# Identity products in TensorE's waits, and a root of eight operations, in a kernel of delta-rule attention and routed experts

## The chip, the cores and the metric

The kernel runs on one core of one Trainium2 chip. The metric is the device time of one execution in microseconds (us), the median of three executions of the same program. The engines are called PE (TensorE matmul), PEld (its weight load), DVE (VectorE), ACT (ScalarE), POOL (GpSimd) and SP (SyncE, which issues DMAs). "Tensor clock" is the clock that the chip grants to TensorE, as the profile shows it: 1.00 is the upper of its two levels (2.4 GHz), 0.50 the lower (1.2 GHz).

## What is computed

A gated delta-rule attention layer over 8 sequences of 512 tokens, width 256, 8 heads of 128, with a small feed-forward behind it, then a layer of 8 experts whose tokens are assigned by 20 rounds of a balanced normalization (Sinkhorn) and of which each token takes two.

```python
# attention layer, x: (8, 512, 256)
q, k = l2norm(silu(h @ Wq)), l2norm(silu(h @ Wk))        # per head, 128 wide
v, beta = silu(h @ Wv), sigmoid(h @ Wb)
alpha = exp(-exp(A_log) * softplus(h @ Wa + dt_bias))
def step(S, t):                                          # S: 128 x 128 per head
    S = S * alpha[t]
    S = S + outer(k[t], (v[t] - k[t] @ S) * beta[t])
    return S, (q[t] @ S) * 128 ** -0.5
o = rms_norm(o) * o_norm_w * silu(h @ Wg)
x = x + o @ Wo
m = rms_norm(x)
x = x + square(relu(m @ W_fc)) @ W_proj
...
# expert layer on layernorm(x), 4096 tokens, 8 experts
la = -(xf @ gate_W.T) / 0.05
for _ in range(20):
    la = la - logsumexp(la, axis=-1, keepdims=True)
    la = la - logsumexp(la, axis=-2, keepdims=True)
pi = exp(la)
_, top_idx = top_k(pi, 2)
y = (silu(xf @ W_gate[e]) * (xf @ W_up[e])) @ W_down[e]
out = sum over k of y[top_idx[:, k]] * pi[:, k]
```

rms_norm, l2norm and layernorm each divide by a square root; the kernel works these out as inverse square roots on DVE and POOL.

## The kernel before

**Staging.** The 4096 tokens are 32 tiles of 128. Start-up loads and norms the input and prepares the decays. Then `step(t, p, more, ahead, tail)` runs once for each tile on every engine: it advances the recurrence of tile t (the "state" part), prepares tile f = t + 1 (the "front" part: projections, transposes, products of keys, the inverse of a triangular matrix in blocks) and finishes tile t - 1 (the "tail": output projection, feed-forward, logits of the gate). Steps 1 to 28 are a loop, the others stand unrolled. In the last step (TILES - 1) there is no next tile, so `more` and `ahead` are false; behind it the tail of tile 31 runs alone. Then come the balanced assignment and the routing (`pe_late`, `dve_late`, `act_late`, `pool_late`), and behind them 24 slots of expert work.

**What sets the order.** Each engine's program is written out by hand; every hand-over is a semaphore. PE runs its instructions in the order of its program, so a wait at one of them holds all behind it.

**The roots.** `root` (L1480) on DVE works out an inverse square root from an integer guess (L1482) and three Newton steps of three operations each (L1484 to L1486): ten operations, each of which waits for the one before (`ch.link`). `k_root` calls it in each step for the norms of the keys of tile f and, in the same instructions, for those of the outputs of tile t - 1; behind it on DVE stand `tail_o` (L1697: o_s times root times gate, which PE transposes at L1991), the scalars of the keys and `delta_products` (L1585: it frees the PSUM bank that PE's next products of keys at L1901 need). `newton` (L1161) does the same on POOL in seven operations for the two norms of a row (`m_root`, `x_root`). For tile 31 both are done by `root` on DVE.

**PE in the last step and after it.** L1957 is the products of the state, L1914, L1929, L1930, L1940 and L1951 the blocks of the inverse, L1991 and L2001 the output projection (tail_o, tail_wo), L2008 and L2018 the first layer of the feed-forward (tail_m, tail_fc), L2028 the second (tail_proj), L2035 and L2042 the logits (tail_xf, tail_logits).

**PE in the assignment and the routing** (`pe_late`). L773 and L775 spread column maxima; L778 is one product for each of the 20 rounds, with the column sums, and DVE does the round's other work (L526 to L531); L780 and L781 count tokens; L787 builds the list of entries in eight batches, from matrices that DVE (L609, L610) and ACT (L749) make; L790 turns it; L797 transposes the first gathered rows of the experts, and from L767 on the experts' products follow.

**Precision.** All these products are 32-bit: a product of `nc.tensor.matmul` on plain f32 data stands in the trace as two records, a transpose or a product of f32r data (L767, L2028) as one.

## Time and profile before

| | us |
|---|---|
| median of 3 runs | 2355.87 (2354.88 to 2356.85) |
| the profiled execution's own time | 2354.47 |
| its span in the trace | 2352.7 |
| PE busy, share of the span | 2130.1 (91%) |
| DVE busy | 1773.0 (75%) |
| ACT busy | 1052.1 (45%) |
| POOL busy | 687.8 (29%) |
| mean granted Tensor clock | 0.956 |

The span is the time from the first to the last instruction in the trace; the execution's own time is 1.8 us more. Busy time is how long an engine works, whatever waits for it; PE's busy time is modelled for pipelined matmuls. In timeline rows the first number is the start, the second how long the row's instructions take together, "x16" how many records they are, and the brackets at the end name the idle time before the row and what ended it.

### The profile page before, as it was taken

The page shows a single profiled execution, that of the slowest core. Times are in us where ns is not written, and L with a number is a line of the kernel's source. Part 1 is how long each engine was busy: PE and PEld are TensorE (multiplying, and loading weights), DVE is VectorE, ACT ScalarE, POOL GpSimd, SP SyncE. Part 2 cuts the span into 40 slices and gives each one's busy share as a digit, 9 for nine tenths or more (in the row PEclk, how much of TensorE's full clock was granted, in tenths as well). Part 3 has the DMA queues.
Part 4 walks back from the last instruction along what each step waited for, and adds up shares of the span by engine and source line. Part 5 has one row for each costly group of instructions (what it writes and reads, how often), then busy time and mean ns, then how long its engine had stood idle before and what let it go on. Part 6 is the DMA issues. An engine that isn't in the chain of part 4 may idle for free. (4 is left out here: it accounts for less than half of the span.)

```text
span 2352.7 us, 50334 instructions
## 1 busy us (share of the span) xinstructions
PE 2130.1 (91%) x16226; PEld 1895.0 (81%) x16226; DVE 1773.0 (75%) x4277; ACT 1052.1 (45%) x2216; POOL 687.8 (29%) x1092
## 2 busy tenths in 40 slices
PE   4679999999999999999999998613799999999998
PEld 4468888888888888888888887512699999999887
DVE  6678888888888888888888887377577666666653
ACT  2334454444444544444445443202455555555542
POOL 0113232332332323323323232000434443344332
PEclk9789999999999999999999999856899999999999
DMA  5321212222222122121221221001444545454331
GB/s 190 114 35 37 57 36 48 44 37 53 39 41 53 36 48 44 37 54 39 43 52 36 48 42 26 8 7 56 153 157 165 188 150 168 143 176 166 125 120 19
DMA packets 307783, 181.71 MB, mean 77 GB/s; under 512 B 244716, under 2 KB 286064, under 8 KB 298512
## 3 DMA queue, kind: packets, MB, share of 16 engines
q1 hardware_dynamic: 255184, 149.21, 22.2%
q0 software_dynamic: 11280, 29.31, 4.4%
q10 hardware_dynamic: 41264, 2.51, 1.1%
q8 instruction: 29, 0.48, 0.1%
q14 instruction: 26, 0.21, 0.0%
HBM read 150.23 MB, written 32.51 MB: 78 GB/s over the span
## 5 line engine op out<-in xcount | busy, mean ns | idle before, releaser
L631 DVE TENSOR_TENSOR w_lo<-w_raw,w_hi 128x512 fp32r<-128x512 f32 x288 | 190.2, 688 | 3.9
L767 PE MATMUL ps_back<-w_hi,eh_hi 128*128 128x256 f32 x624 | 180.0, 289 | 3.2 <-DVE eh_lo L641 3.2
L767 PE MATMUL ps_back<-w_lo,eh_hi 128*128 128x256 f32 x624 | 176.5, 283 | 0.0
L767 PE MATMUL ps_back<-w_hi,eh_lo 128*128 128x256 f32 x624 | 176.4, 283 | 0.0
L721 ACT ACTIVATE w_hi<-w_raw 128x512 fp32r<-128x512 f32 x288 | 169.5, 626 | 0.0
L733 ACT ACTIVATE sact<-ps_inva 128x512 f32<-128x512 f32 (+1 forms) x96 | 49.7, 517 | 236.3 <-PE ps_inva L767 207.1
L1284 ACT ACTIVATE v_s<-ps_front 128x512 f32<-128x512 f32 x64 | 38.1, 595 | 237.9 <-PE ps_front L767 237.9
L1284 ACT ACTIVATE g_s<-ps_front 128x512 f32<-128x512 f32 x64 | 38.2, 598 | 225.8 <-PE ps_front L767 215.8
L1901 PE MATMUL ps_front<-kqT_t 128*128 128x256 f32 x512 | 129.2, 396 | 8.9 <-DVE aP L1585 8.9
L767 PE MATMUL ps_inva<-xT_hi,w_hi 128*128 128x512 f32 (+1 forms) x384 | 135.2, 352 | 1.7 <-DVE xT_lo L636 1.7
L1957 PE MATMUL ps_back<-state,kqT_t 128*128 128x128 f32 x1024 | 132.4, 279 | 3.2 <-DVE r_s L1657 1.7
L767 PE MATMUL ps_inva<-xT_lo,w_hi 128*128 128x512 f32 (+1 forms) x384 | 134.9, 351 | 0.0
L767 PE MATMUL ps_inva<-xT_hi,w_lo 128*128 128x512 f32 (+1 forms) x384 | 134.6, 351 | 0.0
L767 PE MATMUL ps_invb<-xT_hi,w_lo 128*128 128x512 f32 (+1 forms) x384 | 134.2, 349 | 0.0
L767 PE MATMUL ps_invb<-xT_hi,w_hi 128*128 128x512 f32 (+1 forms) x384 | 134.1, 349 | 0.0
L767 PE MATMUL ps_invb<-xT_lo,w_hi 128*128 128x512 f32 (+1 forms) x384 | 134.1, 349 | 0.0
L1957 PEld LDWEIGHTS ps_back<-state,kqT_t 128*128 128x128 f32 x1024 | 126.8, 195 | 6.1 <-DVE r_s L1657 1.9
L659 DVE TENSOR_TENSOR eh<-sact,ps_inva 128x512 f32<-128x512 f32 (+1 forms) x96 | 56.4, 588 | 93.2 <-ACT sact L733 68.3
L2018 PE MATMUL ps_back<-rows,tails 128*128 128x128 f32 x1024 | 126.0, 283 | 0.5 <-ACT rows L1340 0.5
L1187 POOL TENSOR_SCALAR xrow_v<-bag 128x1 f32<-128x1 f32 x31 | 7.1, 228 | 406.7 <-DVE bag L1734 406.7
L1207 POOL TENSOR_TENSOR k_s<-k_s,dbh 128x1024 f32<-128x1024 f32 x32 | 60.7, 1896 | 222.4 <-DVE dbh L1576 222.4
L767 PE MATMUL ps_front<-wqk_hi,hT_hi 128*128 128x512 f32 x256 | 107.3, 419 | 18.9 <-ACT k_s L1284 13.4
(381 smaller groups left out, 6603.2 us busy)
## 6 DMA issues: line engine op xcount, KB each, us to landing
w_raw<-L_ffn_W_gate_dram SPq DMA_DIRECT2D x24, 1024.0 KB
w_raw<-L_ffn_W_up_dram SPq DMA_DIRECT2D x24, 1024.0 KB
w_raw<-L_ffn_W_down_dram SPq DMA_DIRECT2D x24, 1024.0 KB
dT<-alphaT_d SPq DMA_DIRECT2D x32, 512.0 KB, 3.7
x_all<-L_attn_x_dram SPq DMA_DIRECT2D x4, 1024.0 KB, 9.9
hTr<-hT_d SPq DMA_DIRECT2D x32, 128.0 KB, 3.7
lt_d<-aP SPq DMA_DIRECT2D x256, 8.0 KB, 1.5
xi<-low_d SPq DMA_DIRECT2D x32, 128.0 KB
```

The costliest lines, as they stand in the source:

```text
L631: V.tensor_tensor(piece(w_lo[p], m).bitcast(F32R), piece(w_raw, m), piece(w_hi[p], m), ALU.subtract).then_inc(split[n], 1)
L659: V.tensor_tensor(eh[:, s, 0:rows], sact[:, s, 0:rows], psG[2 * s + 1][:, 0:rows], ALU.mult).then_inc(eh_ready[s], 1)
L721: A(piece(w_hi[p], m).bitcast(F32R), piece(w_raw, m), ACT.Copy).then_inc(hi_ready[n], 1)
L733: A(sact[:, s, 0:rows], psG[2 * s][:, 0:rows], ACT.Silu).then_inc(sact_ready[s], 1)
L767: ins = MM(out_, w[a].bitcast(F32R), x[b].bitcast(F32R), start=start and n == 0, stop=stop and n == 2)
L1187: link(pool.tensor_scalar(xrow_v[:, 0:1], bag[:, 1:2], LN_EPS, None, ALU.add), x_pool, n)
L1207: pool.tensor_tensor(k, k, per_head(dbh[:, :]), ALU.mult).then_inc(kd_ready, 1)
L1284: A((k_s[:, q], q_s, v_s, g_s)[n // 2][:, n % 2 * GW:(n % 2 + 1) * GW], psF[u % 2][:, :], ACT.Silu).then_inc(front_evac[u % 2], 1)
L1901: last = MM(ps[:, h * 2 * P:(h + 1) * 2 * P], kqT[:, c, 0, :], kqT[:, c].rearrange("p a n -> p (a n)"), start=True, stop=True)
L1957: last = MM(ps[:, h * DK:(h + 1) * DK], left(g * HG + h), right(g * HG + h), start=True, stop=True)
L2018: last = MM(ps[:, fb * P:(fb + 1) * P], wfc[:, k, c:c + P], mT[:, k * P:(k + 1) * P], start=k == 0, stop=k == KD - 1)
```

## The change

`keep_busy(ps, n)` is new: n products of the identity matrix with itself, 128 x 128 by 128 columns in f32, written to a PSUM bank that nobody reads then. It is put at these places of PE's program, each time ahead of something that PE waits for: in the last step 8 products ahead of block_t, 6 ahead of half_t and 4 ahead of state_out; in tile 31's own tail 22 ahead of tail_o, 16 ahead of tail_m, 4 ahead of tail_proj and 14 ahead of tail_xf; 6 behind tail_logits; in the assignment 10 behind each round's product, 25 more behind the last; 60 behind L781; 35 ahead of the first rows of the experts. That is 400 products.

The root on DVE becomes eight operations instead of ten (another polynomial for the second step); start-up keeps the ten under the name `row_root`. POOL's root becomes six operations instead of seven. The counts of semaphores follow.

```diff
--- before.py
+++ after.py
@@ -59,7 +59,7 @@
 ROOT_MAGIC = 1597463007.0
 LOG_SPREAD = 69.0
 SPREAD = float(np.float32(np.exp(LOG_SPREAD)))
-NEWTON = -8192.0
+NEWTON = -256 / 3
 
 
 NBETA, GAM, GTOT, MEAN = (8 * n for n in range(4))
@@ -301,7 +301,7 @@
 
             return b_filled(s, u) + 1
 
-        N_NORM, N_ROW, N_M, N_O, N_LANE, N_PAIR, N_LATE = 13, 8, 6, 2, 13, 4, 33
+        N_NORM, N_ROW, N_M, N_O, N_LANE, N_PAIR, N_LATE = 11, 7, 5, 2, 13, 4, 27
         N_IDENT, N_ZEROED = 8, 13
         XB16, XB32 = NB16 - 2, NB32 - 1
         N_BLOCKS, N_XBLOCKS = NB16 + NB32, XB16 + XB32
@@ -761,6 +761,10 @@
             for p in range(2):
                 slot(SLOTS - 2 + p, p, BROWS, None if p else BROWS)
 
+        def keep_busy(ps, n):
+            for _ in range(n):
+                nc.tensor.matmul(ps[:, 0:P], ident[:, :], ident[:, :], start=True, stop=True)
+
         def exact(MM, out_, w, x, start, stop):
 
             for n, (a, b) in enumerate(((0, 0), (0, 1), (1, 0))):
@@ -776,9 +780,12 @@
             for n in range(ROUNDS):
                 pe.wait_ge(sk_dve, shares_at(n))
                 MM(col_sums(n), ones[:, :], cols_, start=True, stop=True).then_inc(cols_summed, 1)
+                keep_busy(psI[0][0], 10)
+            keep_busy(psI[0][0], 25)
             pe.wait_ge(rt_dve, 13)
             MM(V3(psF[0][:, 0:TE]), upper[:, :], both, start=True, stop=True).then_inc(rt_pe, 1)
             MM(V3(psF[1][:, 0:TE]), ones[:, :], both, start=True, stop=True).then_inc(rt_pe, 1)
+            keep_busy(psI[0][0], 60)
 
             for b in range(BATCH):
                 pe.wait_ge(lanes_ready, b + 1)
@@ -825,6 +832,7 @@
                     if r % RB == RB - 1:
                         last.then_inc(y_filled[r // RB], 1)
 
+            keep_busy(psI[0][0], 35)
             pe.wait_ge(te_ready, 1)
             rows_T(0, 0, BROWS, BB)
             with pe.Fori(0, SMALL) as i:
@@ -1160,16 +1168,11 @@
             def newton(v, r, a, chain, n):
 
                 first_root(v, r, chain, n + 1)
-                c = 1.0
-                for k in range(3):
-                    m = n + 2 * k + 1
-                    link(pool.tensor_scalar(a, r, r, v, ALU.mult, ALU.mult), chain, m + 1)
-                    last = pool.tensor_scalar(r, a, -3.0 * c * c, r, ALU.add, ALU.mult)
-                    if k < 2:
-                        link(last, chain, m + 2)
-                    c *= -2.0 * c * c
-                assert c == NEWTON
-                return last
+                link(pool.tensor_scalar(a, r, r, v, ALU.mult, ALU.mult), chain, n + 2)
+                link(pool.tensor_scalar(r, a, -3.0, r, ALU.add, ALU.mult), chain, n + 3)
+                link(pool.tensor_scalar(a, r, r, v, ALU.mult, ALU.mult), chain, n + 4)
+                link(pool.tensor_scalar(a, a, -40 / 3, a, ALU.add, ALU.mult), chain, n + 5)
+                return pool.tensor_scalar(r, a, 80.0, r, ALU.add, ALU.mult)
 
             def front_scalars_free(f):
                 pool.wait_ge(ss_ready, 2 * f + 1)
@@ -1185,7 +1188,7 @@
                 pool.sem_inc(pool_turn, 1)
                 n = N_ROW * t + 1
                 link(pool.tensor_scalar(xrow_v[:, 0:1], bag[:, 1:2], LN_EPS, None, ALU.add), x_pool, n)
-                link(newton(xrow_v[:, 0:1], xrow_r[:, 0:1], xrow_r[:, 1:2], x_pool, n), x_pool, n + 7)
+                link(newton(xrow_v[:, 0:1], xrow_r[:, 0:1], xrow_r[:, 1:2], x_pool, n), x_pool, n + 6)
                 pool.tensor_scalar(xrow_r[:, 0:1], xrow_r[:, 0:1], 1.0 / NEWTON, None, ALU.mult).then_inc(xr_ready, 1)
 
             def o_squares(t, p):
@@ -1209,7 +1212,7 @@
             def scaled_v(f):
                 for n in range(2):
                     pool.wait_ge(front_evac[n], f_evac(f, FU_V + n))
-                pool.wait_ge(norm_dve, N_NORM * f + 12)
+                pool.wait_ge(norm_dve, N_NORM * f + 10)
                 pool.sem_inc(pool_turn, 1)
                 pool.tensor_tensor(heads(vb), heads(v_s), per_head(sqk[:, :]), ALU.mult).then_inc(vb_ready, 1)
 
@@ -1480,11 +1483,22 @@
             def root(ch, v, r, a):
 
                 ch.link(V.tensor_scalar(r.bitcast(I32), v.bitcast(I32), -0.5, ROOT_MAGIC, ALU.mult, ALU.add))
+                ch.link(V.scalar_tensor_tensor(a, r, -0.1875, r, ALU.mult, ALU.mult))
+                ch.link(V.tensor_tensor(a, a, v, ALU.mult))
+                ch.link(V.scalar_tensor_tensor(r, a, 0.5625, r, ALU.add, ALU.mult))
+                ch.link(V.scalar_tensor_tensor(a, r, 64 / 9, r, ALU.mult, ALU.mult))
+                ch.link(V.tensor_tensor(a, a, v, ALU.mult))
+                ch.link(V.scalar_tensor_tensor(a, a, -10 / 3, a, ALU.add, ALU.mult))
+                ch.link(V.scalar_tensor_tensor(r, a, 5.0, r, ALU.add, ALU.mult))
+
+
+            def row_root(ch, v, r, a):
+
+                ch.link(V.tensor_scalar(r.bitcast(I32), v.bitcast(I32), -0.5, ROOT_MAGIC, ALU.mult, ALU.add))
                 for _ in range(3):
                     ch.link(V.scalar_tensor_tensor(a, r, -0.5, r, ALU.mult, ALU.mult))
                     ch.link(V.tensor_tensor(a, a, v, ALU.mult))
                     ch.link(V.scalar_tensor_tensor(r, a, 1.5, r, ALU.add, ALU.mult))
-
 
             PART = TILES // XPARTS
             def aggregate(n):
@@ -1513,12 +1527,12 @@
             ch.link(aggregate(XPARTS - 1))
             V.tensor_copy(dec[:, :, MEAN], pmv[:, :, 0])
             ch.link(V.tensor_scalar(pv, pmv[:, :, 1], LN_EPS, None, ALU.add))
-            root(ch, pv, pr, pa)
+            row_root(ch, pv, pr, pa)
             V.tensor_copy(dec[:, :, RINV], pr)
             ch.link(V.tensor_tensor(pms, pmv[:, :, 1], pr, ALU.mult))
             ch.link(V.tensor_tensor(pms, pms, pr, ALU.mult))
             ch.link(V.tensor_scalar(pms, pms, RMS_EPS, None, ALU.add))
-            root(ch, pms, pr2, pa)
+            row_root(ch, pms, pr2, pa)
             ch.link(V.tensor_tensor(phs, pr, pr2, ALU.mult))
             for b in range(BATCH):
                 if b >= 2:
@@ -2056,6 +2070,9 @@
                         transposes(f, FU_TQ, q_s, [g])
                 if more:
                     delta_products(f, 0), delta_products(f, 1)
+                else:
+                    pe.wait_ge(front_evac[0], f_evac(t, FU - 2))
+                    keep_busy(psF[0], 8)
                 block_t(t, p)
                 if tail:
                     tail_o(t - 1)
@@ -2066,6 +2083,8 @@
                 block_xy(t)
                 if more:
                     project(f, q, 4)
+                else:
+                    keep_busy(psF[0], 6)
                 half_t(t, p)
                 if more:
                     project(f, q, 5)
@@ -2080,6 +2099,8 @@
                 state_p(t, p)
                 if more:
                     project(f, q, 6)
+                else:
+                    keep_busy(psF[0], 4)
                 state_out(t, p)
                 if more:
                     project(f, q, 7)
@@ -2113,9 +2134,15 @@
             step(TILES - 3, 1, True, True, True)
             step(TILES - 2, 0, True, False, True)
             step(TILES - 1, 1, False, False, True)
+            keep_busy(psF[0], 22)
             tail_o(TILES - 1), tail_wo(TILES - 1)
-            tail_m(TILES - 1), tail_fc(TILES - 1), tail_proj(TILES - 1)
+            keep_busy(psF[0], 16)
+            tail_m(TILES - 1), tail_fc(TILES - 1)
+            keep_busy(psF[0], 4)
+            tail_proj(TILES - 1)
+            keep_busy(psF[0], 14)
             tail_xf(TILES - 1), tail_logits(TILES - 1)
+            keep_busy(psI[0][0], 6)
             pe_late(pe)
```

On DVE, in the step of tile 29, this is the norm's first part and the root before (the last three rows stand twice more behind it, then comes L1697):

```order
L1544 TENSOR_SCALAR root_v<-ssk 128x8
L1482 TENSOR_SCALAR root_r<-root_v 128x16
L1484 SCALAR_TENSOR_TENSOR root_a<-root_r 128x16
L1485 TENSOR_TENSOR root_a<-root_a,root_v 128x16
L1486 SCALAR_TENSOR_TENSOR root_r<-root_a,root_r 128x16
```

and now, up to `tail_o` (L1711 is L1697 of before):

```order
L1558 TENSOR_SCALAR root_v<-ssk 128x8
L1485 TENSOR_SCALAR root_r<-root_v 128x16
L1486 SCALAR_TENSOR_TENSOR root_a<-root_r 128x16
L1487 TENSOR_TENSOR root_a<-root_a,root_v 128x16
L1488 SCALAR_TENSOR_TENSOR root_r<-root_a,root_r 128x16
L1489 SCALAR_TENSOR_TENSOR root_a<-root_r 128x16
L1490 TENSOR_TENSOR root_a<-root_a,root_v 128x16
L1491 SCALAR_TENSOR_TENSOR root_a<-root_a 128x16
L1492 SCALAR_TENSOR_TENSOR root_r<-root_a,root_r 128x16
L1711 SCALAR_TENSOR_TENSOR o_s<-o_s,root_r,gw 128x128 x8
```

Two operations of the chain are gone; what stands ahead and behind is the same.

On PE, the end of the last step and tile 31's own tail before (the 24 rows of tail_proj, which follow, are left out):

```order
L1957 MATMUL ps_back<-u_s,aP 128x128 x8
L1957 MATMUL ps_back<-u_s,k_s 128x128 x8
L2035 MATMUL ps_back<-ident,rows 128x128 x2
L2042 MATMUL ps_back<-gwT,rows 128x8 x2
L1991 MATMUL ps_back<-ident,o_s 128x128 x8
L2001 MATMUL ps_back<-tails,oT 128x256 x8
L2008 MATMUL ps_back<-ident,rows 128x128 x2
L2018 MATMUL ps_back<-rows,tails 128x128 x16
```

and now (L766 is the product of the identity):

```order
L1971 MATMUL ps_back<-u_s,aP 128x128 x8
L766 MATMUL ps_front<-ident 128x128 x4
L1971 MATMUL ps_back<-u_s,k_s 128x128 x8
L2049 MATMUL ps_back<-ident,rows 128x128 x2
L2056 MATMUL ps_back<-gwT,rows 128x8 x2
L766 MATMUL ps_front<-ident 128x128 x22
L2005 MATMUL ps_back<-ident,o_s 128x128 x8
L2015 MATMUL ps_back<-tails,oT 128x256 x8
L766 MATMUL ps_front<-ident 128x128 x16
L2022 MATMUL ps_back<-ident,rows 128x128 x2
L2032 MATMUL ps_back<-rows,tails 128x128 x16
L766 MATMUL ps_front<-ident 128x128 x4
```

No row of before has moved against another; the products stand between them, ahead of the rows that wait.

On PE, from the column maxima to the experts before:

```order
L773 MATMUL ps_front<-ident,r_s 8x128
L775 MATMUL ps_front<-ident,r_s 128x8
L778 MATMUL ps_back<-r_s,ones 128x8 x20
L780 MATMUL ps_front<-gw,upper 128x256
L781 MATMUL ps_front<-gw,ones 128x256
L787 MATMUL ps_back<-k_s,y 78x128 x8
```

and now, from the last round on:

```order
L782 MATMUL ps_back<-r_s,ones 128x8
L766 MATMUL ps_inva<-ident 128x128 x35
L786 MATMUL ps_front<-gw,upper 128x256
L787 MATMUL ps_front<-gw,ones 128x256
L766 MATMUL ps_inva<-ident 128x128 x60
L794 MATMUL ps_back<-k_s,y 78x128 x8
```

The 35 are the last round's 10 and the 25; the 19 rounds ahead of it have 10 each behind their product.

## Rows read from the trace of the kernel before

**Rows 1.** Busy time by stretch: stretch, length, engines (records), PEclk, DMA share, GB/s
```profile
1453.00:1496.00 43.00, 33.23 (x280) 30.27 (x280) 19.03 (x58) 12.19 (x28) 7.94 (x21) 0.81 0.08 16
1496.00:1535.00 39.00, 19.29 (x92) 16.13 (x92) 16.80 (x64) 8.12 (x14) 1.92 (x4) 0.73 0.04 11
1535.00:1600.00 65.00, 11.28 (x39) 9.49 (x39) 47.60 (x117) 1.66 (x4) 0.00 (x0) 0.50 0.00 0
...
1473.00:1479.00 6.00, 5.12 (x30) 4.68 (x31) 0.35 (x1) 1.14 (x3) 0.26 (x1) 0.50 0.01 3
1497.00:1506.00 9.00, 4.40 (x14) 3.73 (x15) 4.46 (x21) 1.20 (x2) 0.00 (x0) 0.50 0.00 0
```
**Rows 2.** Groups by line, PE, 300 to 1400 us: busy, mean ns, idle before
```profile
L1901 PE MATMUL ps_front<-kqT_t 128*128 128x256 f32 x416 | 103.3, 391 | 5.4 <-DVE aP L1585 5.4
...
L1991 PE MATMUL ps_back<-ident,o_s 128*128 128x128 f32 x208 | 28.3, 279 | 3.7 <-DVE o_s L1697 1.6
```
**Rows 3.** Timeline of one loop step, DVE and PE, from the root on
```profile
901.44 0.17 DVE L1482 TENSOR_SCALAR root_r<-root_v 128x16 int32<-128x16 int32 x1 [0.18 <-DVE root_v L1544]
...
903.53 2.19 DVE L1697 SCALAR_TENSOR_TENSOR o_s<-o_s,root_r,gw 128x128 f32<-128x128 f32 x8
...
905.85 1.09 PE L1991 MATMUL ps_back<-ident,o_s 128*128 128x128 f32 x8
...
907.14 1.13 PE L1901 MATMUL ps_front<-kqT_t 128*128 128x256 f32 x4 [0.20 <-DVE aP L1585]
```
**Rows 4.** Timeline of PE: f32 products at clock 1.00, then at 0.50
```profile
897.79 1.95 PE L1957 MATMUL ps_back<-state,kqT_t 128*128 128x128 f32 x16
...
899.57 1.04 PE L1894 MATMUL ps_front<-ident,k_s 128*128 128x128 f32 x8
...
1628.80 3.67 PE L787 MATMUL ps_back<-k_s,y 128*78 128x128 f32 x16 [19.04 <-ACT y L749]
```
**Rows 5.** Timeline of PE in the last step
```profile
1461.94 0.69 PE L1914 MATMUL ps_inva<-x,aP 32*32 32x32 f32 x32 [1.85 <-DMA x<-x_d]
1462.78 1.97 PE L1991 MATMUL ps_back<-ident,o_s 128*128 128x128 f32 x8
1464.58 4.37 PE L2001 MATMUL ps_back<-tails,oT 128*128 128x256 f32 x16
...
1473.88 0.69 PE L2008 MATMUL ps_back<-ident,rows 128*128 128x128 f32 x2 [2.19 <-DVE rows L1714]
...
1494.89 0.61 PE L2042 MATMUL ps_back<-gwT,rows 128*128 128x8 f32 x4 [0.47 <-ACT rows L1340]
```
**Rows 6.** Timeline of PE in tile 31's own tail
```profile
1501.60 1.97 PE L1991 MATMUL ps_back<-ident,o_s 128*128 128x128 f32 x8 [6.10 <-DVE o_s L1697]
...
1512.36 0.44 PE L2008 MATMUL ps_back<-ident,rows 128*128 128x128 f32 x2 [3.52 <-DVE rows L1714]
1513.27 5.46 PE L2018 MATMUL ps_back<-rows,tails 128*128 128x128 f32 x32 [0.47 <-ACT rows L1340]
...
1527.71 0.69 PE L2035 MATMUL ps_back<-ident,rows 128*128 128x128 f32 x2 [4.54 <-DVE rows L1739]
1528.87 1.02 PE L2042 MATMUL ps_back<-gwT,rows 128*128 128x8 f32 x4 [0.47 <-ACT rows L1340]
```
**Rows 7.** Timeline of a round and of the count, PE and DVE
```profile
1538.18 0.59 PE L778 MATMUL ps_back<-r_s,ones 128*128 128x8 f32 x2 [2.71 <-DVE r_s L531]
1538.89 0.21 DVE L526 RECIPROCAL r_s<-ps_back 128x8 f32<-128x8 f32 x1 [0.76 <-PE ps_back L778]
...
1607.69 1.22 PE L780 MATMUL ps_front<-gw,upper 128*128 128x256 f32 x2 [7.20 <-DVE gw L545]
...
1609.87 0.42 DVE L549 COPY oT<-ps_front 128x256 f32<-128x256 f32 x1 [2.23 <-PE ps_front L781]
```
**Rows 8.** Timeline of PE at the first rows of the experts
```profile
1660.30 1.94 PE L797 MATMUL ps_front<-ident,xrow 128*128 128x128 f32 x8 [9.75 <-issue]
```
**Rows 9.** Timeline of POOL in the last step: one of the root's operations
```profile
1471.13 0.27 POOL L1167 TENSOR_SCALAR mrow_r<-mrow_r 128x1 f32<-128x1 f32 x1 [0.21 <-POOL mrow_r L1166]
```

## The prediction, before the result was known

> **What bounds the kernel now.** I read the busy time by stretch first, then the groups by line of PE in the loop, then the timelines of one step, of the last step and of what follows. Of the loop the reader is to see that PE is never long idle: it waits 5.4 us ahead of L1901 and 3.7 ahead of L1991 in 1100 us [rows 2], 25.7 steps of 42.76 us, so 0.35 us a step. Both waits hang on one chain of DVE: root, L1697, scalars, L1585 [rows 3]. PE bounds the loop but for these. From 1453 to 1664 us it is otherwise: PE is idle for long, waits for chains of DVE, POOL and ACT, and its own work stands in the same chains, at a mean granted clock of 0.81, 0.73 and then 0.50 [rows 1]. There the clock costs time on the path. In the experts (from 1664 us) PE is full at the upper clock, and nothing of the change is there. So there are two gains to price: shorter roots, and products of PE that run at 2.4 instead of 1.2 GHz; and one cost: a row of identity products that is longer than the wait which it fills.
>
> **Prices.** Ten operations of the root take 903.53 - 901.44 = 2.09 us [rows 3], so two are 0.42 us (0.38 for one column, estimated). One operation of POOL's root is 0.27 + 0.21 = 0.48 us [rows 9]. An f32 product is two records; 16 records go in 899.57 - 897.79 = 1.78 us at clock 1.00 and in 3.67 us at 0.50 [rows 4]. An identity product does not stand in the trace; by these it is 0.22 us at the upper clock and 0.46 at the lower. From below 0.21 would be all that the second row halved gives less its end; from above it is 0.24 (1.95 / 16 x 2, with the last one's latency). I take 0.22, the same form and size.
>
> **The loop and the roots: -10.0 us.** The wait at L1901 ends with L1585, that at L1991 with L1697, and both move 0.42 us ahead. L1991 gains its 0.14 us a step (3.7 / 25.7), L1901 its 0.21; PE then comes 0.35 earlier and finds DVE 0.42 earlier, so both waits close. I take 0.33 a step (some switching stays) x 30 steps with a front and a tail: -10.0. The bounds are 0 (another chain is just behind, see the rivals) and 30 x 0.35 = -10.5. What is late next has a slack of only 0.07 us on this chain, so a third operation less would bring nothing more. POOL's roots end before anyone needs them in the loop (no wait of PE for `rows` in rows 2), which I cost at nothing; if that cover went they would be another 0.5 us. The roots of the first two tiles stand ahead of DMA chains in start-up: -0.4 (0 to -0.8).
>
> **The last step: -4.6 us.** PE's 8 products begin at about 1460.1 us and block_t at 1461.94 waits for a DMA [rows 5]: 8 x 0.22 = 1.8 us just fit. Now L1991 and L2001 start at 1462.78 with the clock just fallen, and last until 1464.58 + 4.37 = 1468.95 us: 6.2 us. With the clock held they take 8 x 0.11 = 0.9, half a microsecond for the copy between them, and 16 records of 256 columns at 103.3 / 416 = 0.25 [rows 2] less their overlap, some 3.7: 5.1. That is -1.1, and -0.1 of the root, whose rest the DMA hides. The 6 products (1.3 us) stand ahead of half_t, whose result is needed only behind tail_m, so they delay nobody. POOL's root is one operation shorter: -0.48 at L2008. L2008 to the end of L2018 runs from 1473.88 to 1476.39 + 5.35 us, at 0.50 until 1479 [rows 1, 5]: the upper clock saves 6 of those 6 us' lower-clock work by half, less ACT's own share, -2.6. The 4 products (0.9) fill a wait of 0.8 on DVE ahead of state_out: 0. POOL's second root: 0.48 shorter, of which DVE's state_out leaves -0.25. Sum -4.5, and I take -4.6 with the root of one column behind it hidden; bounds -1.5 (clock falls all the same) and -6.
>
> **Tile 31's own tail: -4.8 us.** The root of L1991's chain: -0.4. Of the 6.10 us of waiting ahead of L1991 [rows 6] 5.7 stay; 22 x 0.22 = 4.8 fit if the clock is high, but PE was idle for most of the 4 us ahead of them, and a part at the lower clock makes them up to 0.6 us late or more. L1991 and L2001 run from 1501.60 to 1512.36 - 3.52 = 1508.84, 7.2 us, at 0.50 until 1506 [rows 1, 6]; held, 5.1. Net -0.4 - 2.1 + 0.6 = -1.9. The 16 products are 3.5 us in a wait of 3.52 that the root shortens to 3.1: the root's 0.4 is lost there. L2018's 32 records take 5.46 us [rows 6] against 32 x 0.11 + 0.2; since ACT and DVE finish the second half behind it, -1.5 of the 1.8 arrive. The 4 products fit in front of hid_ready. The third root -0.4; the 14 products (3.1) fit in 4.54 - 0.4; L2035 and L2042 fall from 0.69 and 1.02 us to 0.44 and 0.61: -0.65; the two small products of the assignment -0.3. Sum -4.8; bounds -1 and -6.5.
>
> **The rounds: -1.3 us.** A round is 3.37 us, of which PE idles 2.71 and DVE waits 0.76 [rows 7]. Ten products are 2.2 us at the upper clock, so they fit, and PE is then busy for most of a round. What the clock gives L778 is in the rows of L2042: four records of 8 columns take 1.02 us at the lower clock and 0.61 at the upper [rows 5, 6], 0.1 a record, so 0.2 for the two of a round: 19 x 0.2 = -3.8. But PE arrives at the first round after a stretch of short products and waits, probably at the lower clock: then ten products are 4.6 us, and the round 0.6 + 4.6 = 5.2, +1.8 us late, once or twice; the break between the two halves of the rounds (DVE and ACT take logarithms for 1.1 us) may cost it again. I take +2.5. Bounds -3.8 and +2.
> The Trainium skill has a rule that speaks against this term (TensorE: Matmul & The Clock Gate, "Single matmul latency"): one product alone takes about (219 + N) / 1.2 ns at the lower clock and (398 + N) / 2.4 at the upper, 189 and 169 ns for N = 8, so the clock hardly shortens a product that someone waits for. By it the 20 rounds would gain some 19 x 0.04 = 0.8 us and the term would be +1.7, an estimate from that page; the trace of L2042 does not agree, 1.02 against 0.61 us, since weight loads are part of it.
>
> **The count, the list, the first rows: -1.0 us.** L780 and L781 take until 1609.87 - 1607.69 = 2.2 us [rows 7], at the upper clock 1.2: -1.0. The 35 products are 7.7 us in a wait of 7.2: +0.5. The 60 are 13.2 us of 19.04 [rows 4]; the other 5.8 us are idle and let the clock fall, so the list begins at 0.50 as before: 0. The 35 behind it are 7.7 of 9.75 us [rows 8]; L797's 8 transposes run at the upper clock (-0.9), but PE then waits again, and the experts begin at the lower one as before, now perhaps for a little longer (+0.4): -0.5.
>
> **The sum.** -10.0 - 0.4 - 4.6 - 4.8 - 1.3 - 0.5 - 0.5 = -22.1 us, against the profiled execution's own time of 2354.47, whose span is 2352.7: 2332.4. That execution lies 1.4 us under the median, so on the median it is 2333.8; I forecast 2334.
>
> **The rivals.** *Only the tail gains.* The loop's wait is taken over by another, the DMAs of block_t above all: in the last step, where nothing else holds PE, it starts only when they land [rows 5], and in the loop PE reaches it hardly later than that. For it speaks how tight that is; against it, that L1914 has no wait in the loop and stands ahead of the two that close. Then 2354.5 - 12 + 1.4: 2344, with half of the loop's gain 2339.
> *Only the roots gain.* The clock falls in spite of the products, for they end before the waits do, and comes late: the products are then twice as long, late at 22, 16 and the rounds. For it speaks that 0.50 stands in all 65 us of the rounds [rows 1]; against it that PE would be busy without a break at those places. Terms: -10.4 - 1.5 - 1 + 2: 2345.
> *Slower.* Products of the identity do not hold the clock at all, as if they were transposes. Each is then 0.46 us and every row of them is late: 19 rounds x 1.8 = +34, 35 products 16.1 in 7.2 us (+9), 60 in 19.0 (+8.5), 35 in 9.75 (+6), 22 in 5.7 (+4.4), 16 in 3.1 (+4.2), 14 in 4.1 (+2.3), the others +3: +71, less 12 of the roots: 2415. It decides as soon as one product takes over 0.27 us, the tenth of the 2.7 us of a round. Against it: at 1508.84 us L1991's transposes and L2001 had been running at 0.50 and the clock had risen, and L787, the same form as the change's products, ends at the upper clock. The Trainium skill states (same page, "PE-mode transpose") that a transpose does not count as busy in the same way; the change's products are plain ones, so by that rule too they should count, and no row here has a long run of transposes alone.
> *It doesn't do what it says*: neither waits nor clock move, within 2 us of 2356.
>
> **How the numbers follow.** The forecast's own case, 2326 to 2338, has 0.60: one end with all bounds of loop and tail (-10.5, -6, -6.5, -3.8, -2), the other with the clock late at half of the places. Only the tail gains: 0.18 (2338 to 2346). Only the roots gain: 0.13 (2341 to 2348). No change 0.04. Slower 0.05. The range from 2326 to 2346 takes in the forecast's case and most of the next two and leaves out under 0.2. About 0.2% (4.7 us) is what a measurement of this kernel can tell from no change. Faster: 0.60 + 0.18 + 0.13 and a little of the next: 0.91; same 0.04; slower 0.05.
>
> **What would show it.** In the changed kernel: L1915 and L2005 of the loop with idle time under 0.1 us a step, steps of 42.43 us; the root in 1.67 us; tenths of the clock at 1.00 in nearly all of the last step, the tail and the rounds; rounds of 3.17 us with 0.56 of waiting on DVE; an identity product at 0.22 us; the list and the first 3 to 6 us of the experts still at 0.50. A step still at 42.7 us proves the loop's term wrong, rounds longer than 3.37 the clock's. If the products take 0.25 us or more, the 22, 16 and 35 are late by 0.5 to 1.5 us each.

## The result, and the profile after

| | before | after |
|---|---|---|
| median, both measured side by side | 2356.18 (2354.88 to 2356.85, 4 runs) | 2329.14 (2327.16 to 2331.65, 4 runs) |
| ratio to before, 95% interval | | 0.9883 [0.9867, 0.9898] |
| the profiled execution, and its span | 2354.47, 2352.7 | 2329.00, 2327.3 |
| PE busy, DVE busy | 2130.1, 1773.0 | 2207.7, 1762.0 |
| mean granted Tensor clock | 0.956 | 0.978 |

The change saves 27.0 us (1.2%). The page of after has these rows on busy time and, in 40 slices, on the clock; PE is busier by 77.6 us, in a kernel that is shorter: 400 products that nobody reads are some 90 us, and what ran at the lower clock before is now shorter. The profile's record of the clock begins at 56.2 us in before and at 34.1 us in after and is taken as 1.00 ahead of that, where the rows of PE go at the lower level; so both means are somewhat too high, before's the more.

```profile
PE 2207.7 (95%) x17026; PEld 1976.3 (85%) x17026; DVE 1762.0 (76%) x4205; ACT 1051.5 (45%) x2216; POOL 664.7 (29%) x1030
...
PEclk8789999999999999999999999999999999999999
```

Busy time by stretch of after, for the last step, tile 31's own tail, the rounds, and what stands between them and the experts; PEclk is the sixth entry. Against [rows 1] the rounds stand at 0.97 instead of 0.50.

```profile
1442.00:1485.00 43.00, 37.95 (x360) 35.33 (x360) 22.76 (x74) 12.08 (x28) 7.18 (x19) 0.94 0.08 17
1485.00:1514.00 29.00, 24.16 (x171) 21.90 (x171) 11.31 (x41) 7.89 (x14) 1.93 (x4) 0.94 0.05 14
1514.00:1576.00 62.00, 53.08 (x418) 49.65 (x418) 47.52 (x117) 1.66 (x4) 0.00 (x0) 0.97 0.01 1
1576.00:1638.00 62.00, 48.77 (x403) 46.66 (x403) 47.51 (x113) 25.83 (x81) 7.88 (x11) 0.94 0.21 67
```

**The loop.** First the groups by line of PE from 300 to 1400 us (busy, mean ns, idle before), the answer to [rows 2], then one step on DVE and PE, the answer to [rows 3].

```profile
L1915 PE MATMUL ps_front<-kqT_t 128*128 128x256 f32 x416 | 103.4, 391 | 0.2
L2005 PE MATMUL ps_back<-ident,o_s 128*128 128x128 f32 x208 | 28.4, 279 | 0.0
```

```profile
897.12 0.17 DVE L1485 TENSOR_SCALAR root_r<-root_v 128x16 int32<-128x16 int32 x1 [0.18 <-DVE root_v L1558]
...
898.80 2.19 DVE L1711 SCALAR_TENSOR_TENSOR o_s<-o_s,root_r,gw 128x128 f32<-128x128 f32 x8
...
901.49 1.66 DVE L1599 SCALAR_TENSOR_TENSOR aP<-ps_front,nbh,dT 128x256 f32<-128x256 f32 x4
```

```profile
901.32 1.09 PE L2005 MATMUL ps_back<-ident,o_s 128*128 128x128 f32 x8
902.42 1.99 PE L1915 MATMUL ps_front<-kqT_t 128*128 128x256 f32 x8
```

The root takes 898.80 - 897.12 = 1.68 us (2.09 before), and both of PE's waits have gone from the groups. The step, from one tile's first product of the state to the next tile's, is 42.33 us instead of 42.76.

**The last step and the tail.** PE of after, from the wait for block_t's DMA on, the answer to [rows 5] and [rows 6]; L766 is the identity product, two records each.

```profile
1448.61 1.95 PE L766 MATMUL ps_front<-ident 128*128 128x128 f32 x16
1450.90 0.69 PE L1928 MATMUL ps_inva<-x,aP 32*32 32x32 f32 x32 [0.34 <-DMA x<-x_d]
1451.53 1.09 PE L2005 MATMUL ps_back<-ident,o_s 128*128 128x128 f32 x8
1452.87 3.72 PE L2015 MATMUL ps_back<-tails,oT 128*128 128x256 f32 x16 [0.25 <-ACT oT L1343]
...
1479.48 5.16 PE L766 MATMUL ps_front<-ident 128*128 128x128 f32 x44
```

```profile
1485.33 1.09 PE L2005 MATMUL ps_back<-ident,o_s 128*128 128x128 f32 x8 [0.69 <-DVE o_s L1711]
1486.67 3.72 PE L2015 MATMUL ps_back<-tails,oT 128*128 128x256 f32 x16 [0.25 <-ACT oT L1343]
1490.23 3.73 PE L766 MATMUL ps_front<-ident 128*128 128x128 f32 x32
1493.80 0.38 PE L2022 MATMUL ps_back<-ident,rows 128*128 128x128 f32 x2
...
1507.10 0.44 PE L2049 MATMUL ps_back<-ident,rows 128*128 128x128 f32 x2 [1.03 <-DVE rows L1753]
```

L2005 and L2015 go at the upper clock in both places, and the waits of 6.10 and 4.54 us of [rows 6] are filled but for 0.69 and 1.03. L2022 has no wait left in front of it: there the 16 products are a little too long (e8 has 14 and comes from L2015's start to this one in 6.86 us instead of 7.13).

**Rounds, count, list.** One round of after on PE and DVE, then PE from the last round to the experts' first rows, the answers to [rows 7] and [rows 8].

```profile
1539.97 0.39 PE L782 MATMUL ps_back<-r_s,ones 128*128 128x8 f32 x2 [0.44 <-DVE r_s L531]
1540.21 2.48 PE L766 MATMUL ps_inva<-ident 128*128 128x128 f32 x20
1540.46 0.21 DVE L526 RECIPROCAL r_s<-ps_back 128x8 f32<-128x8 f32 x1 [0.55 <-PE ps_back L782]
...
1543.13 0.39 PE L782 MATMUL ps_back<-r_s,ones 128*128 128x8 f32 x2 [0.44 <-DVE r_s L531]
```

```profile
1576.29 8.06 PE L766 MATMUL ps_inva<-ident 128*128 128x128 f32 x70
1584.19 0.60 PE L786 MATMUL ps_front<-gw,upper 128*128 128x256 f32 x2
...
1585.06 13.56 PE L766 MATMUL ps_inva<-ident 128*128 128x128 f32 x120
1604.28 3.58 PE L794 MATMUL ps_back<-k_s,y 128*78 128x128 f32 x16 [5.66 <-ACT y L749]
...
1635.51 1.06 PE L804 MATMUL ps_front<-ident,xrow 128*128 128x128 f32 x8 [1.88 <-issue]
```

A round is 1543.13 - 1539.97 = 3.16 us (3.37 before), DVE waits 0.55 for PE in it (0.76 before). Behind the 60 products PE is idle for 5.66 us, and the list begins at the lower clock: 3.58 us, as in [rows 4]. 120 records in 1585.06 to 1598.5 are 13.4 us for 60 products: 0.223 each.

### The profile page after: what moved, and what is told of

Same layout as the page of the kernel before. It is cut to its first block and busy times, and to the rows that moved or that the text cites. A ratio compares the mean times of both kernels' runs of the same rounds, so it can differ in the third digit from the quotient of the medians.

```text
span 2327.3 us, 51622 instructions
## 1 busy us (share of the span) xinstructions
PE 2207.7 (95%) x17026; PEld 1976.3 (85%) x17026; DVE 1762.0 (76%) x4205; ACT 1051.5 (45%) x2216; POOL 664.7 (29%) x1030
## 3 DMA queue, kind: packets, MB, share of 16 engines
q1 hardware_dynamic: 255184, 149.21, 22.3%
## 5 line engine op out<-in xcount | busy, mean ns | idle before, releaser
L771 PE MATMUL ps_inva<-xT_hi,w_lo 128*128 128x512 f32 (+1 forms) x384 | 134.6, 351 | 0.0
L1915 PE MATMUL ps_front<-kqT_t 128*128 128x256 f32 x512 | 127.6, 392 | 3.1 <-DVE aP L1599 2.7
L771 PEld LDWEIGHTS ps_back<-w_hi,eh_hi 128*128 128x128 f32 x624 | 119.5, 191 | 6.0 <-DVE eh_lo L641 5.2
L771 PE MATMUL ps_front<-wqk_hi,hT_hi 128*128 128x512 f32 x256 | 106.9, 418 | 18.4 <-ACT k_s L1287 12.9
## 6 DMA issues: line engine op xcount, KB each, us to landing
hTr<-hT_d SPq DMA_DIRECT2D x32, 128.0 KB, 3.6
xi<-low_d SPq DMA_DIRECT2D x32, 128.0 KB
```

Of the source, the lines that this page charges most:

```text
L771: ins = MM(out_, w[a].bitcast(F32R), x[b].bitcast(F32R), start=start and n == 0, stop=stop and n == 2)
L1915: last = MM(ps[:, h * 2 * P:(h + 1) * 2 * P], kqT[:, c, 0, :], kqT[:, c].rearrange("p a n -> p (a n)"), start=True, stop=True)
```

## The experiments

Every kernel was traced, and the spans were cut at the same events. The step is the mean of steps 3 to 28; "28 to rounds" runs from the start of step 28 to the first round's product, "rounds" from there to the second record of the last round's product, "to experts" from that to the experts' first product. "L1875 ends" is the end of PE's first long row of work in start-up, 128 records with the weights of alpha and beta (L1861 in before). The last column but one leaves start-up out, for a reason that the table itself shows: step 0 began anywhere from 126.4 to 134.7 us, and twice with the same kernel (after) 3.8 us apart.

| kernel | L1875 ends | step 0 at | step | steps 2 to 28 | 28 to rounds | rounds | to experts | experts | step 2 to end | median |
|---|---|---|---|---|---|---|---|---|---|---|
| before | 67.7 | 128.0 | 42.76 | 1112.0 | 209.5 | 65.3 | 63.8 | 688.8 | 2139.3 | 2356.2 |
| after | 73.2 | 130.9 | 42.33 | 1100.7 | 197.4 | 62.0 | 62.2 | 688.8 | 2111.2 | 2329.1 |
| e10, after again | 74.0 | 134.7 | 42.33 | 1100.7 | 198.5 | 63.3 | 62.7 | 688.9 | 2114.1 | 2330.9 |
| e1, roots only | 67.2 | 127.7 | 42.34 | 1101.2 | 202.9 | 65.2 | 63.7 | 688.8 | 2121.8 | 2335.8 |
| e2, products only | 70.7 | 131.3 | 42.77 | 1112.3 | 203.2 | 63.3 | 62.3 | 688.9 | 2130.0 | 2346.4 |
| e3, transposes | 70.7 | 129.9 | 42.33 | 1101.0 | 198.6 | 62.7 | 63.1 | 689.5 | 2114.9 | 2331.5 |
| e4, rounds bare | 73.5 | 132.4 | 42.33 | 1100.9 | 196.7 | 65.1 | 62.5 | 688.8 | 2114.0 | 2331.5 |
| e5, root of 7 | 74.0 | 131.7 | 42.14 | 1096.4 | 196.2 | 63.6 | 62.3 | 689.7 | 2108.3 | 2325.7 |
| e6, root of 9 | 67.8 | 128.3 | 42.55 | 1107.2 | 200.1 | 63.4 | 62.4 | 689.8 | 2122.9 | 2338.8 |
| e7, 16 in a round | 73.4 | 131.9 | 42.34 | 1100.9 | 197.3 | 74.2 | 63.7 | 689.6 | 2125.7 | 2343.3 |
| e8, fitted counts | 73.8 | 134.6 | 42.34 | 1101.7 | 198.3 | 61.4 | 60.4 | 688.4 | 2110.2 | 2328.0 |
| e9, e5 and e8 | 67.6 | 128.0 | 42.13 | 1095.7 | 196.1 | 61.8 | 60.4 | 687.2 | 2101.1 | 2322.0 |
| e11, start filled | 73.9 | 132.6 | 42.33 | 1100.7 | 199.7 | 63.2 | 62.7 | 688.8 | 2115.1 | 2334.7 |
| e12, e9 and e11 | 67.6 | 126.4 | 42.13 | 1095.5 | 196.8 | 61.8 | 60.4 | 687.2 | 2101.7 | 2317.9 |

Before was measured again beside each group, and the ratios go by that: its median was 2358.11 for e1 to e4, 2357.63 for e5 to e8, 2355.19 for e9 to e12. Each row but the median is from one trace.

### e1 and e2: each half alone

The theory gives the loop to the roots and the rounds and the count to the products; the rival has the loop's gain come from something else, or the two halves depend on each other. e1 keeps the roots and drops all products:

```diff
 def keep_busy(ps, n):
-    for _ in range(n):
-        nc.tensor.matmul(ps[:, 0:P], ident[:, :], ident[:, :], start=True, stop=True)
+    return
```

> The changed kernel without any identity product: only the shorter roots. My theory (two gains that add): each loop step is shorter by 0.43 us as in the changed kernel (42.76 to 42.33, 28 steps: -12), the stretch from the last step to the experts is as before but for the roots there (about -2), so about 2342 us against 2356. Rival (the products make the whole gain and the loop's is luck of the start-up): within 3 us of before. PE's granted clock between 1440 and 1660 us is again at 0.50 for most of it.

e2 is the kernel before with all 400 products and its old roots on both engines.

> The kernel before with all 400 identity products and the old roots of ten and seven operations. My theory: the loop is as before (42.76 us a step), the stretch behind it gains 13 us, less the 1 to 2 that the old roots take in it: about 2343 us. With the long roots the waits are longer, so no row of products is late. Rival (the products only pay together with the short roots): under 5 us of gain.

Measured: e1 2335.8 us, 0.9908 [0.9889, 0.9927]; e2 2346.35, 0.9946 [0.9928, 0.9964]. From step 2 to the end the roots alone save 2139.3 - 2121.8 = 17.5 us, the products alone 9.3; the sum, 26.8, lies between the 28.1 and 25.2 of the two traces of after. So the halves add. By the medians they would be 22.3 and 11.8 us (before's was 2358.11 there), more than the whole; the stretches and not the medians of four executions settle it, since start-up scatters. The step is 42.34 in e1 and 42.77 in e2: the loop belongs to the roots. Of the roots' 17.5, 10.9 lie in steps 2 to 28 and 6.6 between step 28 and the rounds; the rounds and the way to the experts are theirs by 0.2 only.

Both expectations were off in the same place. From the last step's start to the first round, 81.2 us in before, the roots alone save 4.4 us where e1's expectation had about 2, and the products alone 5.2. Part of the 4.4 is where the clock happened to fall: it was at the lower level for 36.8 of the 81.2 us in before and for 29.0 of 76.8 in e1, though neither has products; so one trace each does not part the two halves cleanly here. No run parts POOL's shorter root from DVE's either. And in e2 rows of products were late, against its expectation: the 22 took 7.45 us and left no wait, and the first round took 4.85 us.

### e5 and e6: what the loop still waits for

The prediction said that the wait closes with 0.07 us to spare and a third operation less "would bring nothing more". In the trace of after PE shows no idle time there, which seems to agree. The other reading is that the wait is still there and hidden. e5 has a plain second Newton step (seven operations), e6 one multiplication by 1.0 more (nine).

```diff
# e5, behind the integer guess, in place of the seven operations there (left out)
+for _ in range(2):
+    ch.link(V.scalar_tensor_tensor(a, r, -0.5, r, ALU.mult, ALU.mult))
+    ch.link(V.tensor_tensor(a, a, v, ALU.mult))
+    ch.link(V.scalar_tensor_tensor(r, a, 1.5, r, ALU.add, ALU.mult))
 # e6, behind the eight operations
+ch.link(V.tensor_scalar(r, r, 1.0, None, ALU.mult))
```

> The changed kernel with a root of seven operations on DVE (two Newton steps of three operations; less accurate), POOL's as it is. Theory of the lock (each wait of PE that the profile shows is short by the latency of the product ahead of it, and in the changed kernel L1915 still starts 0.05 us behind the end of L1599, so DVE's chain still sets the loop's step): the step falls by up to another 0.2 us, to 42.15, and the loop's 28 steps by up to 5.8 us. Theory of the prediction (both waits are closed, slack 0.07 us): the step stays at 42.33. The three roots behind the loop give 0.5 us in either case.

> The changed kernel with a ninth operation in DVE's root (times 1.0). Theory of the lock: 42.33 + 0.21 = 42.54 us a step, half way back to the 42.76 of before, +5.9 us in 28 steps. Theory of the prediction (slack 0.07): 42.33 + 0.14 = 42.47.

Measured: e5 2325.71 us, 0.9855 [0.9837, 0.9873], its step 42.14; e6 2338.79, 0.992 [0.9904, 0.9937], its step 42.55. One operation less is 0.19 us a step, one more 0.22, with no kink at eight. Both are what the reading of a hidden wait had expected (42.15 and 42.54), and not the prediction's (42.33 and 42.47). The groups of PE for L1915's products, which are L1912 in e5 and L1916 in e6, show why the idle time misleads (groups by line, 300 to 1400 us, first of e5, then of e6):

```profile
L1912 PE MATMUL ps_front<-kqT_t 128*128 128x256 f32 x416 | 102.3, 389 | 0.0
```

```profile
L1916 PE MATMUL ps_front<-kqT_t 128*128 128x256 f32 x416 | 103.4, 391 | 5.4 <-DVE aP L1600 5.4
```

Nine operations and ten [rows 2] show 5.4 us of waiting here alike (with nine the 3.7 us ahead of L1991 are gone), eight and seven nearly none and none, while the step fell by 0.2 us each time. What does not change is the distance from the start of DVE's o_s (L1697 before) to PE's second group of products of keys: before it is 907.14 - 903.53 = 3.61 us [rows 3], in after 902.42 - 898.80 = 3.62. Timeline of DVE and PE in e5, then in e6, then one row of PE in before:

```profile
897.50 2.19 DVE L1708 SCALAR_TENSOR_TENSOR o_s<-o_s,root_r,gw 128x128 f32<-128x128 f32 x8
...
900.22 1.09 PE L2002 MATMUL ps_back<-ident,o_s 128*128 128x128 f32 x8
901.15 1.96 PE L1912 MATMUL ps_front<-kqT_t 128*128 128x256 f32 x8
```

```profile
900.23 2.19 DVE L1712 SCALAR_TENSOR_TENSOR o_s<-o_s,root_r,gw 128x128 f32<-128x128 f32 x8
...
902.55 1.09 PE L2006 MATMUL ps_back<-ident,o_s 128*128 128x128 f32 x8
903.85 1.99 PE L1916 MATMUL ps_front<-kqT_t 128*128 128x256 f32 x8 [0.20 <-DVE aP L1600]
```

```profile
900.45 1.06 PE L1957 MATMUL ps_back<-state,kqT_t 128*128 128x128 f32 x8
```

3.65 and 3.62 us. PE follows DVE's chain at that distance in all four kernels. How much of it is waiting can be read from the starts of PE's rows. From the eight records with o_s to the second group it is 907.14 - 905.85 = 1.29 us with ten operations [rows 3] and 903.85 - 902.55 = 1.30 with nine, 902.42 - 901.32 = 1.10 with eight and 901.15 - 900.22 = 0.93 with seven. Eight records of the same form that nothing holds up need 900.45 - 899.57 = 0.88 ([rows 4] and the last row). So with eight operations PE still waited 0.22 us in each step, none of which is shown as idle, because the modelled end of the matmul ahead covers it. With seven 0.05 is left: a further operation less should bring hardly more than that here, an estimate that no run tried.

### e3: do transposes hold the clock?

The rival "slower" rested on the idea that PE's activity counts by kind. Each product became two transposes of the identity (one record each), so that the number of records stays.

```diff
-for _ in range(n):
-    nc.tensor.matmul(ps[:, 0:P], ident[:, :], ident[:, :], start=True, stop=True)
+for _ in range(2 * n):
+    nc.tensor.transpose(ps[:, 0:P], ident[:, :], ident[:, :])
```

> The changed kernel with each identity product replaced by two transposes of the identity (one record each, so the same two records and 128 columns each), into the same bank. Theory A (what counts is that PE works, as the row 1462 to 1466 us of before with transposes and projections suggested): the clock is held as in the changed kernel, 2329 us. Theory B (transposes do not count, as the Trainium skill states in TensorE: Matmul & The Clock Gate, PE-mode transpose): the clock falls to 0.50 in the last step, tail and rounds, each pair takes 0.46 us instead of 0.22, the rounds are 5.2 instead of 3.16 us and the whole takes about 2400 us.

Measured: 2331.54 us, 0.9888 [0.9872, 0.9905]; from step 2 to the end 2114.9, within 1 us of e10. Two rows of PE in the rounds of e3:

```profile
1536.77 0.39 PE L782 MATMUL ps_back<-r_s,ones 128*128 128x8 f32 x2 [0.53 <-DVE r_s L531]
1537.01 2.38 PE L766 MATMUL ps_inva<-ident 128*128 128x128 f32 x20
```

Twenty transposes take 2.38 us, as long as ten products, and the round's product stays at 0.39. The granted clock was at 1.00 for all rounds but two stretches of 3.4 us, 1514.8 to 1518.2 and 1548.9 to 1552.4, and e10 with plain products has the same two (1520.2 to 1523.6 and 1554.3 to 1557.7). The Trainium skill says that a transpose does not count as busy in the same way and that the full clock does not engage for it (TensorE: Matmul & The Clock Gate, "PE-mode transpose"). These rows do not bear that out: the transposes are 2.38 us of each 3.16, and the other product of a round 0.39.

### e4 and e7: the rounds without products, and with too many

e4 takes the ten products out of each round (the 25 behind the last stay), e7 puts sixteen in.

```diff
 # e4
-    keep_busy(psI[0][0], 10)
 # e7
-    keep_busy(psI[0][0], 10)
+    keep_busy(psI[0][0], 16)
```

> The changed kernel without the 10 products behind each round (the 25 behind the last, and all others, stay). My theory: the rounds run at 0.50 again, 3.37 us each instead of 3.16, so 19 x 0.21 = 4.0 us are lost less the 0.7 us that the first two rounds were late; the count behind them starts with the clock low, and 25 products at 0.46 (11.5 us in a wait of 7.8) are late by 3 to 4 us before the clock rises: about 2335 us. Rival (the clock does not shorten a product of 8 columns, the rounds gain nothing by it): rounds of 3.16 us also here, and a time within 1 us of 2329 plus the count's loss.

> The changed kernel with 16 products behind each round instead of 10. A product goes at 0.225 us (35 of them in 7.9 us), so 16 are 3.6 us and, with the 0.24 of the round's own product, PE's queue of 3.85 us sets the round instead of DVE's chain of 3.16: 19 x 0.69 = +13 us, and +1.3 at the count behind the last: about 2343 us. Rival (PE passes over products whose result nobody reads, or takes them in parallel with the next): rounds stay at 3.16 us.

Measured: e4 2331.46 us, 0.989 [0.9873, 0.9906], its rounds 65.1 us; e7 2343.28, 0.9936 [0.992, 0.9953], its rounds 74.2. Rows of PE, first of e4, then of e7:

```profile
1575.07 0.60 PE L782 MATMUL ps_back<-r_s,ones 128*128 128x8 f32 x2 [2.77 <-DVE r_s L531]
1578.43 0.60 PE L782 MATMUL ps_back<-r_s,ones 128*128 128x8 f32 x2 [2.77 <-DVE r_s L531]
```

```profile
1538.46 0.29 PE L782 MATMUL ps_back<-r_s,ones 128*128 128x8 f32 x2
1538.60 3.82 PE L766 MATMUL ps_inva<-ident 128*128 128x128 f32 x32
1542.26 0.29 PE L782 MATMUL ps_back<-r_s,ones 128*128 128x8 f32 x2
```

Bare rounds are 3.36 us with 0.60 for the product, the numbers of before; ten products in them make 3.16. So their whole gain is 0.2 us a round, 65.1 - 62.0 = 3.1 us at best and 1.8 in e10. Of e4's expectation the rounds came, the late count did not (8.1 us from the last round to L786's product, 8.0 in after): its 25 products took 8.1 us and not 11.5, since the clock rose at 1583.6 us. So e4 is as fast as e10, 2114.0 us from step 2 to the end against 2114.1, and the products in the rounds are the least certain part of the change. e7 came as expected. In e7 nothing waits for DVE any more: a round is 1542.26 - 1538.46 = 3.80 us in these rows, which is 16 products of 0.225 and 0.2 of its own. Nobody reads them and still each is worked off in its place. By these numbers, an estimate that no run tried, twelve would still be free (2.70 us) and thirteen just so: a round leaves 3.16 - 0.24 = 2.92.

### e8 to e10: counts that fit, and both together

After leaves 5.66 us idle ahead of the list and 1.88 ahead of the first rows, and is late at the count and at L2022. e8 changes only the counts:

```diff
+keep_busy(psI[0][0], 1)      # ahead of the wait for the column maxima's second product
...
+keep_busy(psI[0][0], 7)      # behind it
...
-keep_busy(psI[0][0], 25)     # behind the last round
+keep_busy(psI[0][0], 21)
...
-keep_busy(psI[0][0], 60)     # ahead of the list
+keep_busy(psI[0][0], 83)
...
-keep_busy(psI[0][0], 35)     # ahead of the first rows of the experts
+keep_busy(psI[0][0], 43)
...
+keep_busy(psI[0][0], 7)      # behind them
...
-keep_busy(psF[0], 16)        # ahead of tail_m
+keep_busy(psF[0], 14)
...
-keep_busy(psI[0][0], 6)      # behind tail_logits
+keep_busy(psI[0][0], 9)
```

> The changed kernel with other counts: 14 instead of 16 ahead of tail_m, 9 instead of 6 behind the last logits, 1 and 7 new ones around the product of the column maxima, 21 instead of 25 behind the last round, 83 instead of 60 ahead of the list, 43 instead of 35 ahead of the first rows of the experts and 7 new ones behind them. My theory: tail_m 0.3 us and the count 0.5 us earlier, the first rounds without their delay (1.0), the list's first batch at the upper clock (1.9), the experts' first 3.4 us of work at the lower clock gone (1.7): -5 us in the stretch behind 1480 us, with the granted clock at 1.00 all through it. Rival (the experts' and the list's start wait for DMA and ACT, not for PE): -2 us.

Measured: 2327.96 us, 0.9868 [0.9852, 0.9885]. PE of e8 from the count on:

```profile
1588.02 0.70 PE L788 MATMUL ps_front<-gw,upper 128*128 128x256 f32 x2 [0.40 <-DVE gw L545]
...
1588.98 18.70 PE L766 MATMUL ps_inva<-ident 128*128 128x128 f32 x166
1608.20 1.94 PE L796 MATMUL ps_back<-k_s,y 128*78 128x128 f32 x16 [0.52 <-ACT y L749]
```

The list's first batch takes 1.94 us instead of 3.58, and the way from the last round to the experts is 60.4 us instead of 62.2. The median is 1.2 us under that of after, but the two were not measured side by side, and so little is within the scatter of start-up; the gain of 1.8 us stands in the stretch, which e9 and e12 repeat (60.4 both). The -5 us of the expectation did not come: from step 2 to the end it is -1.0 against after and -3.9 against e10, and what is shown, -1.8, is nearer to the rival's -2.

e9 is e5 and e8 together; e10 is after once more, as its reference beside it.

> The changed kernel with both improvements that the experiments pointed to: the root of seven operations on DVE, and the counts of products fitted to the waits (9 for 6 behind the last logits, 14 for 16, 1 and 7 around the column maxima, 21 for 25, 83 for 60, 43 for 35 and 7 more behind the first rows). If the two terms add: steps of 42.14 us (0.2 less than the changed kernel's 42.33, 30 times: -5.8), the stretch from tile 31's L2005 to the end 2.4 us shorter as with the fitted counts alone, together -8: 2321 us, and 2318 to 2325 with the scatter of start-up. If they don't add (the shorter root lets the 22 products come late, or PE becomes the bound of the step): 2325, no better than the root of seven alone.

> The changed kernel once more, as the common reference of this job. Theory: 2329 us, with a start of step 0 anywhere from 128 to 134 us, since that scatter was seen in kernels whose start-up is the same; the stretch from step 2 to the experts as before within 1 us. Rival: the scatter belongs to the kernels and not to the executions; then step 0 starts at 130.9 again, and the time within 0.5 of 2329.1.

Measured: e9 2322.04 us (2317.4 to 2324.1), 0.9858 [0.9843, 0.9873]; e10 2330.88 (2327.59 to 2336.04), 0.9888 [0.9873, 0.9903]. From step 2 to the end e9 needs 2101.1 against 2114.1 and 2111.2: 10 to 13 us less than after. By the medians e9 is 8.8 us under e10, where the two terms added made -8, and it is faster than before and after. By the stretches it is more than the sum of e5 and e8 (-2.9 and -1.0 against after, -5.8 and -3.9 against e10); single traces do not say why. e10 itself missed its expectation: its start of 134.7 us lies beyond the 128 to 134, and the stretch is 2.9 us longer than in the first trace, not within 1. The rival (a start of 130.9 again) is further off. Busy time by stretch in e10, its tail, its rounds and what follows them:

```profile
1491.00:1519.00 28.00, 23.41 (x177) 21.25 (x176) 10.50 (x38) 7.89 (x14) 1.93 (x4) 1.00 0.05 14
1519.00:1583.00 64.00, 54.88 (x422) 51.64 (x422) 48.28 (x118) 1.67 (x5) 0.00 (x0) 0.95 0.01 2
```

And PE of e10 ahead of tile 31's L2005, where the 22 products met the lower clock:

```profile
1483.83 7.83 PE L766 MATMUL ps_front<-ident 128*128 128x128 f32 x44
1491.50 1.04 PE L2005 MATMUL ps_back<-ident,o_s 128*128 128x128 f32 x8
```

The same products took 5.16 us in the first trace of after, with 0.69 to spare; here they take 7.83 and L2005 has no wait: it is late by some 2 us (44.85 us from the last step's start instead of 42.72). The prediction had put that lateness at 0.6. The row of 22 stands in twelve of the traces: in seven it takes 5.16 us and leaves a wait, in five (e10, e2, e3, e6, e9) it takes 6.8 to 7.8 and leaves none.

### e11 and e12: products in start-up

Start-up scatters, and PE's clock in it too. e11 fills three waits there (5.5, 6.1 and 12.9 us) with 20, 24 and 52 products, e12 is e9 with the same.

```diff
+keep_busy(psF[0], 20)
 pe.wait_ge(vg_split, 4 * KD)
...
+for _ in range(24):
+    nc.tensor.matmul(psI[1][1][:, 0:P], ident[:, :], ident[:, :], start=True, stop=True)
 pe.wait_ge(dec_dve, ND_DEC)
...
+keep_busy(psI[1][1], 52)
 project(1, 1, 2)
```

> The changed kernel with identity products in three waits of PE in start-up too: 20 ahead of the first projection (a wait of 5.5 us), 24 between the decays' products and their transposes (6.1 us) and 52 ahead of the last projection before step 0 (12.9 us). Theory (the lower clock in start-up makes its length and its scatter): step 0 starts at 126 to 128 us instead of 130.9, with 20 us or less of the lower clock behind the first projection instead of 37, and the time is 3 us shorter, 2326. Rival (start-up hangs on ACT, DVE and DMAs, and PE's clock only follows): step 0 starts at 130 or later, since products at the lower clock (52 of them 24 us in a wait of 12.9) are late by up to 11 us there: 2330 to 2340.

> The root of seven, the fitted counts and the products in start-up together. If all three terms add: 2321 - 3 = 2318 us. If the products in start-up are late: 2322 to 2332, with the loss all before step 0.

Measured: e11 2334.66 us (2330.11 to 2336.0), 0.9903 [0.9887, 0.9918]; e12 2317.86 (2313.94 to 2321.47), 0.9837 [0.9823, 0.9852]. Of the pair e11 and e10 the filled one is 3.8 us slower, of the pair e12 and e9 it is 4.2 us faster, and the intervals overlap within each pair: no verdict. e12 hits the 2318 that was expected and e11 is in the rival's range, but neither for its reason. The traces say more. What splits them happens ahead of the first of the added products. PE of after in start-up, then PE of e12, the same work:

```profile
56.31 3.43 PE L1875 MATMUL ps_back<-wba,y 128*128 128x16 f32 x16
...
66.33 3.43 PE L1875 MATMUL ps_back<-wba,q_s 128*128 128x16 f32 x16
```

```profile
56.85 1.86 PE L1877 MATMUL ps_back<-wba,y 128*128 128x16 f32 x16
...
64.01 3.57 PE L1877 MATMUL ps_back<-wba,rows 128*128 128x16 f32 x16
```

PE works from 36 to 37 us on without a break in all fourteen traces. In five (before, e1, e6, e9, e12) the clock rises at 56.1 to 56.7 us, falls again at 63.0 to 63.5 with PE still at work, and this row of work ends at 67.2 to 67.8; in seven it stays at the lower level to the end, which is at 73 to 74; in e2 and e3 it is up for 3.4 us only, and the row ends at 70.7. In e5, e8, e10 and e11 the profile has no record of the clock until 79 us or later and shows 1.00 for this time; there the level is read from the rows, 3.43 us for 16 records as in after at 0.50. The table's first two columns go together: where L1875 ends at 67 to 68, step 0 begins at 126 to 128; where it ends at 73 to 74, at 131 to 135. That is most of the scatter, and it is one of TensorE's clock, at a place where none of the added products stands; the rest lies behind that row (57.7 to 60.8 us to step 0). From the end of L1875 to step 0 it was 58.7 and 58.8 us in e11 and e12, 60.7 and 60.4 in their partners e10 and e9, but 57.7 and 57.8 in after and e5, which have no products there. The products did hold the clock: between the row's end and step 0 it was low for 10 us in e12 and 37 in e9. What that brings is at most 2 us, and not shown. Products in PE's idle first 30 us, ahead of this row, would be the next thing to try; that wasn't tried.

## Why the prediction was right, and where it was off

The forecast was 2334 us in a range of 2326 to 2346; 2329.14 is within it and 4.9 us below the forecast. Against the median of before the sum of -22.1 was -27.0. By its steps:

- **The loop, -10.0 forecast, -11.3 from step 2 to 28, -13.7 from step 2 to the last step's start.** This is the term that was mis-sized, and the only one where a reason was wrong; it makes 4 of the 6.4 us by which the stretch from step 2 on beat the forecast. The mechanism was right: e1 has all of it, e2 none, and the root takes 1.68 us. But the step lost 0.43 us, all of the two operations, and not 0.33. The prediction read PE's idle time (0.35 us a step, 0.21 of it at L1901) as the size of the wait, and got a slack of 0.07 from it. The wait at L1901 was 1.29 - 0.88 = 0.41 us, half of it under the modelled end of the matmul ahead. "A third operation less would bring nothing more" is refuted by e5: another 0.19 a step, 1100.7 - 1096.4 = 4.3 us in steps 2 to 28.
- **The last step and tile 31's own tail, -4.6 and -4.8.** From the last step's start to the first round it went from 81.2 to 71.5 us, -9.7 against -9.4, and in e10 -8.4. By the start of the logits' product in the last step, -4.8 and -4.9 in after. The 8 products fit (0.34 us of the DMA's wait left), and L2005 and L2015 take 1.09 and 3.72 us, as worked out. The 22 were in time in after and 2 us late in e10, the 16 about 0.3 us too long. So the sums were right, but who brings them is not as forecast: the terms give the roots some 1.6 us of it (0.1, 0.48, 0.25, 0.4, 0.4), and e1 shows 4.4 with roots alone, part of it by where the clock fell. That the total came out to 0.3 us is in part luck, as the 1.3 us between after and e10 show.
- **The rounds, -1.3.** -3.2 in after, -2.0 in e10 and in e2. The price of a round was right (3.16 us against 3.17, DVE's wait 0.55 against 0.56), the +2.5 for lower clock too dear for after: the first round was late by 0.5 us, 3.66 instead of 3.16 (1514.13 to 1517.79 us), and the break between the halves kept the upper clock. In e10 the first round is 1.0 late and the clock fell in the break too (1554.3 to 1557.7 us), another 0.8; in e2 and e5 the first round takes 4.85 us, +1.7, as priced. One product at the lower clock was priced at 0.46 us from 3.67, which has the last record's end in it; from L787's first row to the next (1628.80 to 1632.27 us) it is 3.47, so 0.43. The Trainium skill's rule for one matmul (TensorE: Matmul & The Clock Gate, "Single matmul latency"), stated there for bf16, would have given 0.04 us a round for these two f32 records, an estimate. The trace gives 0.21, and e4 takes it away again. To leave the rule out was right.
- **The count, the list, the first rows, -1.0.** 8.01 us from the last round to L786 instead of 7.56 (+0.45; +0.5 was forecast), 20.09 instead of 21.11 from L786 to the list (-1.0, as forecast), the list still at 0.50 (as forecast), and from the list to the experts' first product -1.0 in after and -0.5 in e10, where -0.5 was forecast.
- **Start-up, -0.4.** Not to be seen: step 0 began 2.9 us later in the profile of after than in that of before, with code that differs only in the key's root. e10 shows 134.7 for the same kernel. The profiled execution of before happened to be one in which the clock rose for a while in start-up, and that of after one in which it didn't; by such scatter, and not by a better term, the forecast is 4.9 us off by the medians where it is 6.4 off from step 2 on. This scatter, 8 us between the extremes of fourteen traces, is larger than most terms of the sum, and medians of few executions carry it; from step 2 on, the forecast's -21.7 stands against -28.1 and -25.2.

Of the rivals, "only the tail gains" falls by e1 (-10.8 us in the loop), "only the roots gain" by e2 (-9.3 us) and by the clock in the stretches. "Slower" named its point well: it decides when the products of a round are longer than the wait, which e7 brought about by their number (+12.2 us in the rounds, against after) since the clock did not. But that transposes would not hold the clock is not so (e3).

## What to carry to other kernels

A short chain of small operations that a full engine waits for is worth its whole length for as long as the engine starts at a fixed distance behind it: compare that distance in two kernels, not the idle time shown. Products that nobody reads are worth putting into waits of PE where PE's own work stands in the chain and would run at the lower clock; count them by 0.22 us at the upper clock, leave half a microsecond, and measure at more than one execution, since the same 22 took 5.2 us in seven traces and up to 7.8 in five, where the clock had fallen. Too few leave a gap in which the clock falls again (60 ahead of the list, with 5.66 us idle; 83 held it), too many are paid in full (16 in a round).

## What the runs showed of the hardware

- An f32 identity product of 128 x 128 by 128 columns took 0.223 to 0.225 us at the upper clock (60 in 13.4 us, 16 in a round of e7).
- A product of two records of 8 columns takes 0.39 us at the upper (after) and 0.60 at the lower clock (e4), where someone waits for it. Its two weight loads take 0.30 and 0.50 us of PEld there, so the weight load changes with the clock.
- Transposes held the clock as products did (e3: 20 of them in 2.38 us of each 3.16, clock 1.00 in all but 6.8 us of the rounds, as in e10 with products).
- In start-up PE worked without a break from 36 to 37 us on. The clock rose at 56 to 57 us and fell again at 63 in five executions, was up for 3.4 us in two, and did not rise before the end of that work, at 73 to 74 us, in seven, where the work ends 6 us later than in the five. Nothing in the traces tells why the one or the other.
- A wait of PE can be larger than its idle time: the eight records with o_s and the next group start 1.10 us apart in after, with no idle time in their rows, where 0.88 is enough.
